# Layer 0 of a two-layer decoder: VectorE's normalizations and key products cut into more, shorter steps between attention slots, and GpSimd's roots moved behind the slot's diagonals

## Reference

```python
x = _layernorm(x + _L0_attn_ref(x, ...))        # softmax over one head: every weight is 1, so a sum over tokens
x = _layernorm(x + _L0_xattn_ref(x, ctx, ...))  # 16 heads; 3x3 convolution of the masked scores, then softmax
x = _layernorm(x + _L0_ffn_ref(x, ...))         # rmsnorm, 16-head causal attention with a normalized latent and
                                                # rotary embedding, rmsnorm, and one of 4 experts per token
```

```python
attn = q @ k.T * scale; attn0 = where(mask, 0, attn)
attn = conv3x3(attn0, kernels[b, head]); attn = where(mask, -inf, attn); out = softmax(attn) @ v @ proj_W + proj_b
```

## Time and profile before

| | |
|---|---|
| median of three runs | 2574.84 us (2568.9 to 2577.97) |
| the profiled execution | 2571.01 us |
| its span, first to last instruction | 2569.2 us |
| mean granted TensorE clock over the span | 0.888 |
| busy: TensorE, VectorE, ScalarE, GpSimd | 2203.8, 1340.0, 995.6, 362.7 us |
| layer 0 with its attentions | about 154 to 1130 us |
| near blocks 2, 3 and 4 begin at | 331, 440 and 549 us |

### The profile page before, as it was taken

The page is one execution under the profiler, slowest core; times in us unless marked ns, Lnnn a source line. Parts: engine busy times, 40 slices in busy tenths (PEclk is TensorE's granted clock), DMA queues, the critical chain, the costliest instruction groups (busy, mean ns, idle before and its releaser), DMA issues. The chain is left out here.

```text
span 2569.2 us, 38948 instructions
## 1 busy us (share of the span) xinstructions
PE 2203.8 (86%) x13569; PEld 1547.9 (60%) x13637; DVE 1340.0 (52%) x3927; ACT 995.6 (39%) x3145; POOL 362.7 (14%) x639
## 2 busy tenths in 40 slices
PE   8588888889999987897727789899999999999887
PEld 4266665656777764676514456566666666766654
DVE  7245556464635454321149457565656565666441
ACT  3133535445454534352212245444434344444320
POOL 2044252332504142001000000000000000000000
PEclk9767989888899978997859699999999999999988
DMA  8000000001233111445550000000000000000000
GB/s 305 9 5 1 5 5 10 9 9 32 97 103 106 44 38 51 154 175 194 166 168 0 15 10 5 6 5 10 5 5 10 5 10 5 6 5 5 5 1 9
DMA packets 50763, 116.27 MB, mean 45 GB/s; under 512 B 8192, under 2 KB 30464, under 8 KB 46976
## 3 DMA queue, kind: packets, MB, share of 16 engines
q1 hardware_dynamic: 49024, 109.49, 12.6%
q0 software_dynamic: 1536, 4.20, 0.5%
HBM read 90.20 MB, written 23.46 MB: 44 GB/s over the span
## 5 line engine op out<-in xcount | busy, mean ns | idle before, releaser
L690 ACT ACTIVATE PRS<-PT 128x384 f32<-128x384 f32 (+1 forms) x512 | 266.1, 520 | 653.7 <-PE PT L621 653.5
L755 DVE TENSOR_REDUCE negmax<-SM 128x2 f32<-128x512 f32 x432 | 283.5, 685 | 194.3 <-PE SM L584 96.7
L621 PE MATMUL PT<-const_sb,PRS 128*128 128x128 f32 x1664 | 309.6, 304 | 51.7 <-ACT PRS L690 49.5
L705 ACT ACTIVATE PRS<-SM,negmax 128x128 f32<-128x128 f32 x608 | 248.1, 420 | 184.8 <-DVE negmax L755 184.8
L621 PEld LDWEIGHTS PT<-const_sb,PRS 128*128 128x128 f32 x1664 | 206.1, 153 | 147.6 <-issue 97.6
L2758 DVE TENSOR_SCALAR arena<-arena 128x256 bf16<-128x256 bf16 x1024 | 210.3, 279 | 9.9 <-PE SC L2776 9.0
L574 PE MATMUL SM<-haloU,QM 32*128 32x128 f32 (+1 forms) x1056 | 172.9, 376 | 7.1 <-ACT PRS L705 4.7
L574 PEld LDWEIGHTS SM<-haloU,QM 32*128 32x128 f32 x1056 | 131.2, 216 | 22.8 <-ACT PRS L705 8.6
L2776 PE MATMUL SC<-arena,identb 128*128 128x256 bf16 x1024 | 138.2, 278 | 2.4 <-DVE arena L2758 2.4
L636 PE MATMUL OA<-PRS,big 128*32 128x256 f32 (+1 forms) x1024 | 133.7, 387 | 3.0 <-ACT PRS L690 3.0
L574 PE MATMUL SC<-haloU,QM 32*128 32x128 f32 (+1 forms) x480 | 111.3, 388 | 28.3 <-ACT PRS L705 28.3
(11 more groups left out here) (565 smaller groups left out, 4072.3 us busy)
## 6 DMA issues: line engine op xcount, KB each, us to landing
arena<-lay SPq DMA_DIRECT2D x50, 1024.0 KB, 4.9
arena<-lay SPq DMA_DIRECT2D x1, 7700.5 KB, 21.4
rows<-OT SPq DMA_DIRECT2D x2, 3456.0 KB, 32.4
arena<-lay SPq DMA_DIRECT2D x1, 3862.0 KB, 20.6
arena<-rows SPq DMA_DIRECT2D x25, 128.0 KB, 2.6
arena<-lay SPq DMA_DIRECT2D x25, 128.0 KB, 5.1
rows<-arena SPq DMA_DIRECT2D x25, 128.0 KB, 4.4
rows<-OT SPq DMA_DIRECT2D x1, 2432.0 KB, 21.3
```

What stands on the lines that cost most here:

```text
L621: ins = pe.transpose(bank[:, o:o + P], PR[n % 4][:, t, k * P:(k + 1) * P], ident)
L690: act.activation(dst, src, ACT.Copy).then_inc(S("probs_moved"), 1)
L705: ins = act.activation(dst, src, ACT.Exp, bias=negmax[:, h, r:r + 1], accum_out=rsum[:, t, h:h + 1])
L755: st.post(dve.tensor_reduce(negmax[:, ORDER[s], :], two(banks[s % NB]), AX.X, ALU.max, negate=True), S("max_ready"))
```

## The change

No computation is added or removed; steps are split and moved.

- `layernorm` becomes `variance` (moments and `var`) and `normalized` (wait for the root, multiply). In `open_dve` a `yield` stands between the two. In `layernorm_rmsnorm` (of `join`) and `rmsnorm` (of `judge`) a `yield` stands ahead of the wait for the root. So `open`, `join` and `judge` get one step more: OPEN 4 to 5, JOIN 4 to 5, JUDGE 3 to 4.
- In `turn` the number of steps stays 7: VectorE's step 0 keeps the copy of the latent and its variance; the multiplication by the root and by `ln_g` go behind the cosine product of step 1, the addition of `ln_b` behind the sine product and the sum of step 2.
- `keys` goes from 5 to 7 steps: the six taps of the first key half are split in three and three, with the copy of `kfac` behind the first three and the diagonal factors behind the second three; the nine products of the second half are split in six and three.
- GpSimd's roots stand one step later in `open`, `join`, `turn` and `judge`, and thus behind the diagonals of the slot in which VectorE multiplies. TensorE, ScalarE and SyncE get empty steps, so that a step that uses the result stands behind it: TensorE turns the normalized rows in step 4 of `open` and of `join` (before: 3).

```diff
-        def layernorm(dve, st, w, dst, src, n, flag=None):
+        def variance(dve, st, w, src):
             moments(dve, st, w, src)
             st.post(dve.tensor_scalar(w.var[:], w.mv[:, :, 1], 1.0, LN_EPS, ALU.mult, ALU.add), w.var_ready)
+            st.settle()
+
+        def normalized(dve, st, w, dst, src, n, flag=None):
             dve.wait_ge(w.rstd_ready, n)
             for t in range(TT):
                 st.post(dve.tensor_scalar(dst[t], src[t], w.mv[:, t, 0:1], w.rstd[:, t:t + 1],
                                           ALU.subtract, ALU.mult), flag)
...
             st.post(dve.tensor_scalar(square[:], square[:], 1e-6, None, ALU.add), S("square_ready"))
+            st.settle()
+            yield
             dve.wait_ge(w.rstd_ready, n)
...
             st.post(dve.tensor_scalar(w.var[:], small[:, 100:102], 1.0, 1e-6, ALU.mult, ALU.add), w.var_ready)
             st.settle()
+            yield
             dve.wait_ge(w.rstd_ready, n)
...
-        OPEN, KEYS, JOIN, TURN, JUDGE = 4, 5, 4, 7, 3
+        OPEN, KEYS, JOIN, TURN, JUDGE = 5, 7, 5, 7, 4
...
-            layernorm(dve, st, norm_a, token_tiles(Xi), token_tiles(Xi), i + 1, S("x_ready"))
+            variance(dve, st, norm_a, token_tiles(Xi))
+            yield
+            normalized(dve, st, norm_a, token_tiles(Xi), token_tiles(Xi), i + 1, S("x_ready"))
...
                 dve.wait_ge(S("first_taps"), 3 * (i + 1))
-                for j in range(1, 3):
-                    for a in range(3):
-                        st.post(tap(0, a, j), S("kc_ready"))
-                    st.settle()
+                for a in range(3):
+                    st.post(tap(0, a, 1), S("kc_ready"))
+                st.settle()
                 bank = bp.take(dve, "dve")
                 bp.release(st, dve.tensor_copy(kfac[:], bank[:, 0:TT * 3 * H].rearrange("p (t j h) -> p t j h", t=TT, j=3)), "dve")
                 st.settle()
+            yield
+            if mode == "near":
+                for a in range(3):
+                    st.post(tap(0, a, 2), S("kc_ready"))
+                st.settle()
                 diagonal_factors()
             yield
...
-                for j in range(1, 3):
-                    for a in range(3):
-                        st.post(tap(1, a, j), S("kc_ready"))
-                    st.settle()
+                for a in range(3):
+                    st.post(tap(1, a, 1), S("kc_ready"))
+                st.settle()
+            yield
+            if mode == "near":
+                for a in range(3):
+                    st.post(tap(1, a, 2), S("kc_ready"))
+                st.settle()
             yield
...
-            layernorm(dve, st, norm_m, token_tiles(lat), token_tiles(lat), 2 * i + 2)
-            st.settle()
-            for t in range(TT):
-                st.post(dve.tensor_tensor(lat[:, t, :], lat[:, t, :], w0("ln_g"), ALU.mult))
-            st.settle()
-            for t in range(TT):
-                st.post(dve.tensor_tensor(lat[:, t, :], lat[:, t, :], w0("ln_b"), ALU.add), S("lat_ready"))
-            st.settle()
+            variance(dve, st, norm_m, token_tiles(lat))
             yield
...
             times(w0("cos"), QFc[:, :, 1:T + 1])
+            normalized(dve, st, norm_m, token_tiles(lat), token_tiles(lat), 2 * i + 2)
+            st.settle()
+            for t in range(TT):
+                st.post(dve.tensor_tensor(lat[:, t, :], lat[:, t, :], w0("ln_g"), ALU.mult))
+            st.settle()
             yield
             times(w0("sin"), Y[:])
             st.post(total(QFc), S("q_rotated"))
+            for t in range(TT):
+                st.post(dve.tensor_tensor(lat[:, t, :], lat[:, t, :], w0("ln_b"), ALU.add), S("lat_ready"))
             st.settle()
...
         def turn_pool(pool, i):
 
+            yield
             root_pool(pool, norm_m, 2 * i + 2)
-            yield from idle(TURN)
+            yield from idle(TURN - 1)
...
         def judge_pool(pool, i):
 
-            yield from idle(2)
+            yield from idle(3)
             root_pool(pool, norm_e, i + 1)
             yield
```

More of the change, by code:

```diff
@@ L430, in layernorm @@
                                           ALU.subtract, ALU.mult), flag)
+        def layernorm(dve, st, w, dst, src, n, flag=None):
+            variance(dve, st, w, src)
+            normalized(dve, st, w, dst, src, n, flag)
         def layernorm_rmsnorm(dve, st, w, dst, scaled, src, weight, n, rms_n):
@@ L1267, in open_act @@
         def open_act(act, sa, i, bp):
-            yield from idle(3)
+            yield from idle(4)
             bank = bp.take(act, "act")
@@ L1307, in keys_pe @@
                 bp.fill(ins, "dve")
-            yield
-            yield
+            yield from idle(4)
         def keys_act(act, sa, mode, i, b, bp):
@@ L1326, in keys_act @@
                                    scale=head_taps(b)[:, 0, 3 * a:3 * a + 1]).then_inc(S("first_taps"), 1)
-            yield
-            yield
-            yield
+            yield from idle(5)
         def keys_dve(dve, st, mode, i, b, bp):
@@ L1486, in join_dve @@
             bank = bm.take(dve, "dve")
-            layernorm_rmsnorm(dve, st, norm_m, token_tiles(X2s[i % 2]), token_tiles(XM), tiles(bank), w0("norm1"), 2 * i + 1, i + 1)
+            yield from layernorm_rmsnorm(dve, st, norm_m, token_tiles(X2s[i % 2]), token_tiles(XM), tiles(bank), w0("norm1"), 2 * i + 1, i + 1)
             st.settle()
@@ L1601, in judge_dve @@
                 dve.wait_ge(S(f"y_out{i % 2}"), 16 * (i // 2))
-            rmsnorm(dve, st, norm_e, token_tiles(Zg[i % len(Zg)]), tiles(bank), w0("norm2"), i + 1, S("zn_ready"))
+            yield from rmsnorm(dve, st, norm_e, token_tiles(Zg[i % len(Zg)]), tiles(bank), w0("norm2"), i + 1, S("zn_ready"))
             for t in range(TT):
```

1 line of the change is left out of this document (added).

## The result

The changed kernel takes 2507.3 us, the median of four runs (2501.89 to 2515.65), beside 2574.68 for the kernel before on the same chip. The ratio, made from the rounds in which both ran, is 0.9742 with a 95% interval of 0.9708 to 0.9775: 2.6% faster. The forecast was 2528, 1.8% faster, with 2510 to 2560 as its range. So the direction held and the size did not: 67 us gained where 47 were forecast. Four later runs of the same program on another chip gave 2498.89 to 2519.98 (median 2513.79), and all eight have a median of 2509.9, at the range's lower end.

A forecast was written before the change was run, and what follows sets the result against it. TensorE, busy 86%, was taken to bound the kernel, through its waits and lowered clock. From 2571.0 us, 22.2 of waits and 24.5 of clock leave 2524.3; 3.8 more for the median gives 2528, whole range 2510 to 2560.

The forecast's parts named there:

- The clock: TensorE's half-clock stretches vanish: 7 us in each of near blocks 2 to 4, 3.5 in blocks 0 and 1, sum 24.5.
- (a): Near blocks 2 to 4, slot 3: splitting `judge`'s normalization cuts TensorE's wait from 3.01 to 0.56 us, 7.3 in all.
- (b): Near blocks 2 to 4, slots 0 and 1: `turn`'s shorter step 0 removes waits of 0.60 and 0.94, 4.6 us.
- (c): Near blocks 2 to 4, slots 6 and 7: splitting `open`'s layernorm removes a wait of 1.27, 3.8 us in all.
- (d): Near blocks 0 and 1: splitting `open`'s layernorm cuts waits of 3.40 and 3.77 to 0.56 each, 6.0 us.
- (e): Fine block 6: the wait of 2.98 behind `join`'s double normalization falls to 0.56, 2.4 us.
- (f): Fine blocks 0 to 5, `keys` in seven steps: three smaller waits replace one of 2.62, 1.4 us gained.
- (g): Costs: 0.3 us at block 1's first near scores and 3.0 for steps colliding in fuller slots, 3.3 subtracted.
- The clock stays: Rival, chance 0.22: the waits go but the half clock in the near blocks remains, only 22.2 us gained, 2553 us.
- The wait moves: Rival, chance 0.08: near blocks' fuller slots are late by what was saved, TensorE waits one slot on, 2575 us.
- VectorE bounds the fine blocks: Rival, chance 0.08: slots 5 to 7 of fine blocks 0 to 5 grow, costing 56 us against 34 gained, 2597 us.

The follow-up runs named there:

- `judge_root_early`: The changed kernel with GpSimd's root of `judge` alone put back in step 2, VectorE's normalization still split: 2536.84 us, ratio 0.9877.
- `judge_whole_late`: The changed kernel with VectorE's normalization of `judge` whole in one step again (all batches but one), its root left late: 2537.0 us, ratio 0.9859.
- `join_whole`: The changed kernel with `join`'s double normalization whole in step 2 again, its 5 steps kept: 2530.74 us, ratio 0.9831.
- `join_six`: The changed kernel with one empty step added in `join` ahead of its normalization, to part it from `keys` in slot 4: 2516.7 us, ratio 0.9758.
- `judge_pad`: The changed kernel with `judge`'s moments of the first three batches taken three times, 2.2 us more VectorE work, nothing moved: 2529.34 us, ratio 0.9854.

## Why the prediction was wrong

**The step that failed is the extent in "The clock".** The waits were forecast at 22.2 us, and TensorE's idle time in layer 0 fell by 20.9. That the sums agree so well is in part luck: near block 0 came out with 1.5 us more idle time where 2.8 less was forecast, and near block 7 and fine block 6 gave 2.4 and 4.0 where 0 and 2.4 stood. The clock was forecast at 24.5, and TensorE's busy time fell by 41.2. The prediction took the one long stretch at half clock in near blocks 2 to 4 and half of two more: 59.8 us of half clock, and wrote "The clock of other stretches I leave". Summed over the clock's records of layer 0, the time at half went from 293.7 to 197.5 us, so by 96.2. The price of such time was right: 7 us for 17.1 is 0.41 for each, and 41.2 of 96.2 is 0.43. By the Trainium skill, "TensorE: Matmul & The Clock Gate", section "Terms", half of it is lost, an estimate of 48.1. Over the layer the row's price was the nearer, and the page's is too high by a sixth. In near blocks 2 to 4 alone it is the other way round: 61.4 us at half fewer and 29.0 us of busy time, 0.47 for each. With the extent that was taken neither price fills the gap of 16.7.

Where the extent was missed can be read from the stretches. Of the 96.2 us, 61.4 lie in near blocks 2 to 4 (51.3 taken; the missing stretches of 3.4 us stood only in the range's lower bound), 13.5 in near blocks 0 and 1 (8.5 taken), 17.1 in near block 7 (none taken), and 4.2 elsewhere. A near block's clock of 0.84 over 63.2 us is 20 us at half, not 17.1, and it went to 1.00: 9.7 us of busy time in near block 3, 29 in three such blocks, where 21 were forecast; 20 us at the forecast's own price would have made it 25. Near block 7 (0.81 to 0.92) gave 4.5 us of busy time and 2.4 of idle, and near blocks 0 and 1 together 7.8 of busy time where 3.5 stood.

**From the layer to the median.** 15.3 us more than forecast came from layer 0 (62.0 at its end, against 46.7). Layer 1, which nothing touched, took 6.6 back in the profiled execution, and it varies with the clock from execution to execution. The rest is the executions' scatter: the forecast added 3.8 for the median over the profiled time, and the changed kernel's median was 8.4 below its own. 15.3 - 6.6 + 12.2 = 20.9, beside the 20.7 us by which the forecast was off.

By its own steps:

- (a) Right in size, incomplete in cause. The wait went from 3.01 to 0.62, so by 2.4 of 2.45. But the step gave all of it to VectorE and spoke of GpSimd's root as 0.37 us. `judge_root_early` and `judge_whole_late` show two causes side by side, either of which holds the wait up by itself.
- (b) Right as to the waits: those of 0.60 and 0.94 are gone. The slot from 0 to 1 fell from 8.6 to 4.8 and that from 1 to 2 grew from 4.7 to 7.0, together 1.5 us less, which is what was forecast. But put back whole, `turn` costs 3.4 to 4.9 us in each of near blocks 2 to 4, with 3.4 to 6.8 us of half clock, for which the forecast had nothing.
- (c), (d) The wait of 1.27 in near block 3 and that of 0.56 ahead of it are gone, but one of 0.42 between them is 1.35 now: 0.9 less, where 1.27 was forecast. With (a)'s 2.4 and (b)'s 1.5 that is the block's 4.8 us of idle time. The waits of 3.40 and 3.77 in near blocks 0 and 1 are 0.56 and 0.97 now, about as forecast. In the chain behind near block 0 a wait grew that the forecast left out: 5.97 us for `join`'s double normalization, where it was 1.96, with 1.48 for the key products. The 50 us that `open`'s parts cost when they are put back are another quantity than the 9.8 us of waits (and 3.5 of clock) forecast for them: they are priced in the new layout, where the layernorm lies a slot earlier than it did.
- (e) The wait of 2.98 is gone, and one of 0.95 stands a slot earlier. Fine block 6 and the chain behind it are 5.5 us shorter, forecast 2.4.
- (f), (g) The fine blocks 0 to 5 grew by 4.1 in sum, where -1.4 and up to +3.3 were forecast. In fine block 2 the wait of 2.62 became waits of 1.02 and 0.67, near what (f) worked out, but its clock went from 0.93 to 0.85. What (f) left out is slot 4, where `keys`' step 3 and `join`'s moments now meet (before: slots 6 and 5): the slot from 4 to 5 takes 8.1 to 14.3 us in the six fine blocks, where it took 3.5 to 6.3, and the one from 5 to 6 3.8 to 6.1, where it took 8.0 to 8.9. Fine block 3 has a wait of 3.40 us that was not foreseen. VectorE's rows there show `route`'s chain of small instructions between `join`'s moments and the maxima:

```profile
590.45 0.17 DVE L450 TENSOR_SCALAR square<-square 128x2 f32<-128x2 f32 x1
590.65 0.15 DVE L1752 TENSOR_TENSOR arena<-gate_s 1x4 f32<-1x4 f32 x1
...
592.84 0.17 DVE L1776 CAST ids_i<-arena 1x18 int32<-1x18 f32 x1
593.03 0.69 DVE L767 TENSOR_REDUCE negmax<-SM 128x2 f32<-128x512 f32 x1
```

- `join` in fine blocks 0 to 5 stood at nothing. With the split undone they are 14 us longer, so the change's layout needed it, though against the kernel before it shows as no gain. Of this step what was shown ahead has to be corrected: GpSimd's root of `join` stays in step 2, and only an empty step is added behind it. In a fine block no diagonals stand behind that root.
- The prediction read near blocks 2 to 4 as alike to within 0.1 us; by the row maxima they took 63.1, 63.2 and 63.5. Nothing hangs on it.

**The rivals.** "The clock stays" is refuted: near blocks 2 to 4 run at 1.00 (in the second trace with 6.8 us at half in block 2). "The wait moves" is refuted for the changed kernel (0.62 us ahead of slot 4), though it is what `join_six` met. "VectorE bounds the fine blocks" had the right place and the wrong size, 4 us and not 56.

What stays open: what `open`'s and `turn`'s long steps with late roots would each cost in all, why near block 6 has two lengths, and what the seven steps of `keys` are worth, which the scatter of 2499 to 2520 hides.

## What to carry to other kernels

A small operation that waits for another engine (here a root of 0.70 us) holds all that stands behind it in its own queue, so it belongs behind the work that others wait for; and where VectorE's step and GpSimd's root are late together, repairing either alone gains little (in `judge` nearly nothing, over all three 15 and 28 us of 87), while the profile names only the one that ended last. Price a change of the clock over every block whose waits go, by the block's granted clock, and not by its longest stretch. One step more in a braided schedule moves all others, so undoing a part afterwards prices it in the new layout and not against the kernel before.

## What was unexpected in the hardware

- Short waits were enough to bring the clock down. In `judge_pad` a wait of 2.18 us stands in a stretch with 6.8 us at half; with 0.62 us there the clock stayed full. A change of 1.6 us in three waits was worth 14 us.
- One program takes different ways through the clock. In its two profiled executions near block 0 takes 75.3 and 81.2 us and near block 2 48.7 and 51.6. Near block 0 of the second, with the columns of the earlier trace rows, has as many matmuls as the first and a clock of 0.69, where the first had 0.75:

```profile
155.40:236.60 81.20, 68.98 (x412) 49.48 (x413) 38.70 (x89) 27.30 (x93) 38.43 (x73) 0.69 0.01 4
```

- Near block 6 takes 73.9 to 75.5 us in some kernels and 78 to 82 in others, among them `join_whole`, which has no work of `join` in that block. Single blocks can't be compared between two kernels from one trace each.
